# Query rotation inside the projection's bank, and routing logits from the product that turns a tile back

## The reference, cut to what matters

```python
h = _layernorm(x) * (1 + ca) + sa
q = rmsnorm(einsum('bim,mhd->bhid', h, wq)); k = rmsnorm(einsum('bim,mhd->bhid', h, wk))
even, odd = split(q, 2, axis=-1)                       # the same for k
q = concatenate([even * cos - odd * sin, even * sin + odd * cos], axis=-1)
p = softmax(q @ k.T / 128 + causal mask); x = x + ga * (p @ v @ wo)
h = _layernorm(x) * (1 + cb) + sb
scores = softmax(h @ Wr + br); top_idx = top_k(scores, 2)
weights = softmax(where(chosen, scores, -inf))
x = x + gb * sum_e(weights_e * (gelu(h @ W1_e + b1_e) @ W2_e + b2_e))
```

## Time and profile before

| | |
|---|---|
| median of three runs | 1145.86 us (1144.65 to 1147.39) |
| span of the profiled execution, first to last instruction | 1104.4 us |
| PE busy | 1019.0 us, 92% |
| ScalarE busy | 969.8 us, 88% |
| VectorE busy | 923.8 us, 84% |
| GpSimd busy | 825.8 us, 75% |
| mean granted clock of PE | 0.969 |

### The profile page before, as it was taken

How to read it: one execution, slowest core, us unless ns; L and a number is a source line. 1 busy time by engine, 2 the same in 40 slices (tenths; PEclk the granted TensorE clock), 3 DMA queues, 4 the chain that set the end, 5 groups by cost and what they waited for, 6 DMA issues and landing times. The chain is left out here.

```text
span 1104.4 us, 27346 instructions
## 1 busy us (share of the span) xinstructions
PE 1019.0 (92%) x7434; PEld 791.3 (72%) x7434; DVE 923.8 (84%) x2706; ACT 969.8 (88%) x3517; POOL 825.8 (75%) x1197
## 2 busy tenths in 40 slices
PE   5899999999999999999999999999989999999800
PEld 3478888888888888888888888888865455579600
DVE  4888999989999999888888888888766997778837
ACT  6899999999999999999999999999769999999534
POOL 6665578888888888888878788888745687777744
PEclk9999999999999999999999999999999999999955
DMA  5320000001000000000000000000034233321158
GB/s 150 104 71 14 13 18 23 23 26 34 27 23 26 26 23 14 16 16 16 14 15 16 14 14 16 16 16 16 16 111 129 84 118 104 96 85 40 46 207 261
DMA packets 53704, 57.90 MB, mean 52 GB/s; under 512 B 7964, under 2 KB 42639, under 8 KB 53556
## 3 DMA queue, kind: packets, MB, share of 16 engines
q1 hardware_dynamic: 36468, 35.10, 10.9%
q0 software_dynamic: 8640, 16.87, 4.4%
q10 hardware_dynamic: 8448, 4.20, 1.3%
HBM read 33.08 MB, written 23.97 MB: 52 GB/s over the span
## 5 line engine op out<-in xcount | busy, mean ns | idle before, releaser
L751 ACT ACTIVATE squares<-unit 128x128 f32<-128x128 f32 x1024 | 273.0, 302 | 3.6 <-PE unit L1211 3.4
L563 POOL TENSOR_TENSOR roped<-roped,rope_b 128x512 f32<-128x512 f32 x132 | 174.9, 1326 | 93.8 <-DVE rope_b L1099 91.4
L751 ACT ACTIVATION_READ_ACCUMULATOR squares<-unit 128x1 f32 x1024 | 234.1, 235 | 0.0
L1080 DVE TENSOR_TENSOR roped<-unit,cos_sb 128x512 f32<-128x512 f32 x256 | 174.4, 681 | 31.7 <-ACT squares L751 30.9
L1563 POOL DMA_INDIRECT y_rows<-y_out,place_y x142 | 155.3, 1093 | 54.3 <-issue 40.5
L1099 DVE TENSOR_TENSOR rope_b<-unit,sin_sb 128x512 f32<-128x512 f32 x256 | 174.3, 681 | 0.0
L729 ACT ACTIVATE probs<-scores,rr 128x256 f32<-128x256 f32 x256 | 123.7, 483 | 51.6 <-issue 25.5
L1291 PEld LDWEIGHTS unit<-ident,roped 128*128 128x128 f32 x1024 | 117.9, 142 | 31.9 <-ACT k_t L768 13.1
L1049 DVE SCALAR_TENSOR_TENSOR acc<-pv,den,acc 128x128 f32<-128x128 f32 x448 | 139.0, 341 | 0.3
L1291 PE MATMUL unit<-ident,roped 128*128 128x128 f32 x1024 | 135.2, 275 | 1.7 <-POOL roped L563 1.6
L572 POOL TENSOR_TENSOR roped<-roped,rr 128x1024 f32<-128x1024 f32 x64 | 121.6, 1900 | 9.6 <-DVE roped L1108 8.8
(11 more groups left out here) (310 smaller groups left out, 2972.3 us busy)
## 6 DMA issues: line engine op xcount, KB each, us to landing
shared<-y_rows SPq DMA_DIRECT2D x16, 512.0 KB, 5.6
x_all<-in_L_attn_x SPq DMA_DIRECT2D x32, 128.0 KB, 2.1
h_late<-in_L_ffn_W SPq DMA_DIRECT2D x16, 256.0 KB, 3.5
out_x<-hidden ACTq DMA_DIRECT2D x16, 256.0 KB, 4.4
rope_b<-x_rows SPq DMA_DIRECT2D x13, 258.0 KB, 2.9
tile_x<-x_rows SPq DMA_DIRECT2D x12, 258.0 KB, 3.0
y_rows<-y_out,place_y POOLq DMA_INDIRECT x142, 2.3
ga_b<-mod_dram SPq DMA_DIRECT2D x32, 64.0 KB, 2.9
```

What stands on the lines that cost most here:

```text
L563: pool.tensor_tensor(out=roped[parity][:, u, heads], in0=roped[parity][:, u, heads], in1=rope_b[:, u % 2, heads], op=ALU.add)\
L751: nc.scalar.activation(squares[:, c * D:(c + 1) * D], UN[0][:, c * D:(c + 1) * D], ACT.Square, accum_out=ssq[parity][:, u * H + c:u * H + ...
L1080: nc.vector.tensor_tensor(out=roped[parity][:, u, heads].rearrange("p (g c) -> p g c", c=D // 2), in0=UN[0][:, heads].rearrange("p (g c) - ...
```

## The change

For queries from pass 1 on, VectorE makes the sines first, then writes the cosine products back over the projection in its PSUM bank, and adds that bank and `rope_b` into `roped`. PE's projection waits for that add (`q_added`) two steps on, for steps 2 to 5. Keys, and pass 0, stay as they were.

The tile `ident_wr` holds the identity and, beside it, the routing weights. One f32 product of each tile of `h2_t` with these 136 columns gives the rows and the logits together, in steps 1 and 2 (`ROUTED`), beside the values products of heads 0 and 1. The turns of steps 4 and 5 and the group of one-row and 8-column products go. VectorE adds the bias, held in all partitions in `br_all` (one more load), to each tile's logits into the old place in `OP[0]` (`BIASED0`, `BIASED1`). Its later routing steps move: the maxima and `LESS_TOP` from step 1 to 2, `E_SUM` and `E_REC` from 3 to 4, some of the next by a slot; ScalarE's exponential moves from step 2 to 3, and GpSimd's score behind its low part of `h`. The diff leaves out the names of semaphores and most unchanged lines.

```diff
--- before.py
+++ after.py
@@ -84,7 +84,8 @@
         b_t = sb("b_t", [P, E * FC + E])
-        ident = sb("ident", [P, P])
+        ident_wr = sb("ident_wr", [P, P + E])
+        ident, wr_sb = ident_wr[:, 0:P], ident_wr[:, P:P + E]

@@ -96,10 +97,8 @@
         mod_t = sb("mod_t", [P, 4, NB])
-        wr_sb = sb("wr_sb", [P, E])
         br_sb = sb("br_sb", [1, TT * E])
-        br_rest = [sb(f"br_rest{k}", [1, TT * E]) for k in range(2)]
-        br_part = [sb(f"br_part{k}", [1, TT * E], BF16) for k in range(3)]
+        br_all = sb("br_all", [P, E])
         ones_row = sb("ones_row", [1, P])
@@ -293,7 +292,7 @@

-        (TOP_L0, TOP_L1, LESS_TOP, E_SUM, E_REC, TOP_S0, TOP_S1, TOP_I0, TOP_I1, ONE_HOT) = range(1, 11)
+        (BIASED0, BIASED1, TOP_L0, TOP_L1, LESS_TOP, E_SUM, E_REC, TOP_S0, TOP_S1, TOP_I0, TOP_I1, ONE_HOT) = range(1, 13)
         STEPS = ONE_HOT
@@ -302,8 +301,9 @@
         XN_AT, XN2_AT = 2, 3
-        BESIDE, TURN_AT = 2 * P + 8, 3 * P
+        BESIDE, TURN_AT = 2 * P + 8, 3 * P - E
         BACK_AT = {H_AT: 1, H_AT + 1: 0}
+        ROUTED = {1: 0, 2: 1}
         HH = H // 2
@@ -391,6 +391,8 @@
                     .then_inc(S["router_in"], 16)
+            sp.dma_start(br_all[:, :], br.rearrange("(o e) -> o e", o=1).broadcast_to([P, E]))\
+                .then_inc(S["router_in"], 16)
             sp.dma_start(b_rows[0:E * FC, :], b1.rearrange("e (k p) -> (e k) p", p=P)).then_inc(S["b_in"], 16)
@@ -626,18 +628,18 @@
                     scatter(n - 6, parity, 0, 0)
+                if X:
+                    b = n + 1
+                    wait(pool, "hhi_done", b + 1)
+                    wait(pool, "vw_done", TT * (b - 1))
+                    pool.tensor_tensor(out=h_lo[other][:, :], in0=h_t[:, :], in1=h_hi[other][:, :], op=ALU.subtract)\
+                        .then_inc(S["h_ready"], 1)
                 if RT:
...
                                        op=ALU.mult).then_inc(S["scored"], 1)
-                if X:
-                    b = n + 1
-                    wait(pool, "hhi_done", b + 1)
-                    wait(pool, "vw_done", TT * (b - 1))
-                    pool.tensor_tensor(out=h_lo[other][:, :], in0=h_t[:, :], in1=h_hi[other][:, :], op=ALU.subtract)\
-                        .then_inc(S["h_ready"], 1)
                 if A:
@@ -775,7 +777,7 @@
                             .then_inc(S["guess_done"], 1)
-                    if RT and h == 2:
+                    if RT and h == 3:

@@ -817,8 +819,7 @@
                         if not late:
-                            wait(act, "rt_done", b)
-                            wait(act, "h2_back", TT * b)
+                            wait(act, "rt_done", TT * b)
                         nc.scalar.activation(h2_late[:, b - LAST, :] if late else h2_t[:, :], UN[1][:, 0:T],
@@ -879,21 +880,13 @@

-                dve.wait_ge(S["router_in"], 16 * (TT + 1))
-                nc.vector.tensor_copy(br_part[0][:, :], br_sb[:, :]).then_inc(S["br_parted"], 1)
-                for k in range(2):
-                    whole = br_rest[0] if k else br_sb
-                    dve.wait_ge(S["br_parted"], 2 * k + 1)
-                    nc.vector.tensor_tensor(out=br_rest[k][:, :], in0=whole[:, :], in1=br_part[k][:, :],
-                                            op=ALU.subtract).then_inc(S["br_parted"], 1)
-                    dve.wait_ge(S["br_parted"], 2 * k + 2)
-                    nc.vector.tensor_copy(br_part[k + 1][:, :], br_rest[k][:, :]).then_inc(S["br_parted"], 1)
+                dve.wait_ge(S["router_in"], 16 * (TT + 2))
                 dve.wait_ge(S["b_turned"], 1)
...
             ROUTE = {
-                (1, 0): (TOP_L0, TOP_L1), (1, 1): (LESS_TOP,), (3, 3): (E_SUM,), (3, 4): (E_REC,),
-                (5, 0): (TOP_S0, TOP_S1), (5, 1): (TOP_I0,), (5, 2): (TOP_I1,),
+                (1, 1): (BIASED0,), (2, 0): (BIASED1,), (2, 1): (TOP_L0, TOP_L1), (2, 3): (LESS_TOP,),
+                (4, 0): (E_SUM,), (4, 1): (E_REC,), (5, 1): (TOP_S0, TOP_S1), (5, 2): (TOP_I0,), (5, 3): (TOP_I1,),
                 (6, 1): (ONE_HOT,)}
@@ -956,10 +949,14 @@
                     lg = OP[0][:, BESIDE:BESIDE + TT * E].rearrange("p (t e) -> p t e", t=TT)
-                    if step in (TOP_L0, TOP_L1):
+                    if step in (BIASED0, BIASED1):
+                        t = step - BIASED0
+                        wait(dve, "rt_done", TT * b + t + 1)
+                        ins = nc.vector.tensor_tensor(out=lg[:, t, :], in0=OP[t][:, TURN_AT + P:TURN_AT + P + E],
+                                                      in1=br_all[:, :], op=ALU.add)
+                    elif step in (TOP_L0, TOP_L1):
                         t = step - TOP_L0
-                        if t == 0:
-                            alone(dve, "rt_done", b + 1)
+                        after(BIASED0 + t)
                         ins = nc.vector.max(top_l[:, t, :], lg[:, t, :])
@@ -1020,7 +1017,7 @@
                     b, t = n - 5, BACK_AT[h]
-                    wait(dve, "h2_back", TT * b + h - H_AT + 1)
+                    wait(dve, "rt_done", TT * b + t + 1)
                     if (not isinstance(b, int) or b >= 2) and h == H_AT:
@@ -1064,34 +1061,23 @@
                     heads = slice(bank * HH * D, (bank + 1) * HH * D)
-
-                    adds, ended = (C, (n - 2, h - 1)) if h else (R, (n - 3, H - 1))
-                    if adds:
-                        denominators(*ended)
-                    small(h, 0)
-                    if ST and h == 2:
-                        place_e_step()
-                    if ST and h == 3:
-                        place_step()
-                    if A:
-
-                        wait(dve, "sq_done", HH * (w + 1))
-                        wait(dve, "tr_done", NU * (n - 1))
+                    in_place = h < HH and n > 0
+
+                    def cosines():
+
+                        if in_place:
+                            wait(dve, "rope_done", w + 1)
+                        else:
+                            wait(dve, "tr_done", NU * (n - 1))
+                        turned = UN[0][:, heads] if in_place else roped[parity][:, u, heads]
                         nc.vector.tensor_tensor(
-                            out=roped[parity][:, u, heads].rearrange("p (g c) -> p g c", c=D // 2),
+                            out=turned.rearrange("p (g c) -> p g c", c=D // 2),
                             in0=UN[0][:, heads].rearrange("p (g c) -> p g c", c=D // 2),
...
                             op=ALU.mult).then_inc(S["ropea_done"], 1)
-                    small(h, 1)
-                    if adds:
-                        add_head(*ended, 0)
-                    small(h, 2)
-                    if RT and h in BACK_AT:
-                        copy_rows(h)
-                    if adds:
-                        add_head(*ended, 1)
-                    small(h, 3)
-                    if A:
+
+                    def sines():
+
                         if h < HH:
@@ -1102,11 +1088,39 @@
                             op=ALU.mult).then_inc(S["rope_done"], 1)
-                    if A and h < HH and n > 0:
-
-                        wait(dve, "rope_done", w + 1)
-                        nc.vector.tensor_tensor(out=roped[parity][:, u, heads], in0=roped[parity][:, u, heads],
+
+                    adds, ended = (C, (n - 2, h - 1)) if h else (R, (n - 3, H - 1))
+                    if adds:
+                        denominators(*ended)
+                    small(h, 0)
+                    if ST and h == 2:
+                        place_e_step()
+                    if ST and h == 3:
+                        place_step()
+                    if A:
+                        wait(dve, "sq_done", HH * (w + 1))
+                        if in_place:
+                            sines()
+                        else:
+                            cosines()
+                    small(h, 1)
+                    if adds:
+                        add_head(*ended, 0)
+                    small(h, 2)
+                    if RT and h in BACK_AT:
+                        copy_rows(h)
+                    if A and in_place:
+                        cosines()
+                    if adds:
+                        add_head(*ended, 1)
+                    small(h, 3)
+                    if A and in_place:
+                        wait(dve, "ropea_done", w + 1)
+                        wait(dve, "tr_done", NU * (n - 1))
+                        nc.vector.tensor_tensor(out=roped[parity][:, u, heads], in0=UN[0][:, heads],
                                                 in1=rope_b[:, u % 2, heads], op=ALU.add).then_inc(S["q_added"], 1)
+                    elif A:
+                        sines()
                     small(h, 4)
@@ -1223,11 +1237,15 @@
                     o, pr, v = OP[h % 2], probs[:, h % NPR, :], vals[parity]
-                    if RT and h + 1 in BACK_AT:
-                        t = BACK_AT[h + 1]
+                    if RT and h + 1 in ROUTED:
```

(69 more changed lines are left out.)

6 lines of the change are left out of this document (1 added, 5 removed).

## The result

| | before | after |
|---|---|---|
| median, both kernels side by side | 1146.62 us (1144.17 to 1155.59, 8 runs) | 1134.12 us (1131.1 to 1142.35, 8 runs) |
| ratio | | 0.990 (0.987 to 0.993) |
| the same on a later occasion | 1106.15 us (15 runs) | 1094.35 us (4 runs) |
| ratio there | | 0.990 (0.988 to 0.991) |
| late logits start (end of attention) | 813.41 us | 801.42 us |

The change saves 1.0%: 12.5 us by the medians here, 11.8 on the later occasion. It lies in attention: the late logits start 12.0 us earlier.

A forecast was written before the change was run, and what follows sets the result against it. PE's instruction stream was taken to bound the attention pass: 0.56 us saved, less 0.17 at head 7 and 0.03 at LESS_TOP, left 0.36 to 0.38. 28 x 0.38 = 10.6 us off 1145.86 gave 1135.2 us, range 1130 to 1146.

The forecast's parts named there:

- PE's stream bounds the pass, and the net of its products is 0.56: Attention loop: a pass is as long as PE's instructions; 0.81 + 0.22 - 0.47 = 0.56 us less a pass.
- Wide products: PE, steps 1 and 2: two f32 products of 136 columns, 0.235 us each, 0.47 together.
- Late next is the accumulation of head 5, and it costs 0.17: Before head 7's values product PE waits 0.11 us for VectorE's accumulation and shows 0.06 of weight load.
- Cosines over the bank: VectorE, query rotation: writing into the bank costs between -0.01 and +0.1 us extra for 512 columns; 0 taken.
- rival C: Query rotation: reading and writing one bank takes 0.53 us extra; +5 us in all, 1151; chance 0.11.
- D: Rival, wide products: four 0.11 us steps a tile, 0.88 in all; 4 us saved, 1142; chance 0.03.
- LESS_TOP: VectorE, head 2: done 2.32 us after the reciprocal, PE needs it by 2.41; stall 0 to 0.15, 0.03 taken.
- The release of the projection's bank: Projection of head 5: bank released later, with the query add, at 526.62; in time by 0.3 us, 0 in the sum.
- None of this is on the path: in heads 0 to 3 VectorE waits for PE or ScalarE anyway.: Query rotation on VectorE, heads 0 to 3: its changed operation times do not affect the pass; 0 taken.
- rival A: VectorE not late, gaining more from adds no longer sharing SBUF with POOL: 16 to 17 us, 1129; chance 0.17.
- VectorE works without a gap through heads 4 to 6: VectorE, from 527.31 until head 5's accumulation ends: unbroken work, 0.25 us earlier, that accumulation moving from 534.27 to 534.02.
- the 41.5 us: Whole kernel: difference between span 1104.4 us and median 1145.86, taken as fixed time around the span.

The follow-up runs named there:

- the repeat: The whole change run once more on the later occasion, against the kernel before: 1094.35 us, ratio 0.990, passes of 24.16 us.
- the delayed kernel: The changed kernel with three added 128x8 copies on VectorE in front of LESS_TOP in head 2: 1134.76 us, 1.026 of the kernel before.
- rotation alone: The kernel before with only the query rotation through the bank, routing as before: 1106.59 us, ratio 1.001, passes of 24.57 against 24.56.
- ONE_HOT late: The changed kernel with ONE_HOT moved behind the accumulation of head 5: 1091.02 us, 0.987 of the kernel before, passes of 24.00.

## Why the prediction held, point by point

**Right.** *PE's stream bounds the pass, and the net of its products is 0.56*: with the edge at head 7 cleared, passes fall by 24.56 - 24.00 = 0.56. *Wide products* at 0.235 each: 0.23 for the first; the second shows 0.31 to what follows, but the extra 0.08 stood in the same place before, behind the first values product of head 1 (519.70 to 520.00 in the kernel before). *Waits on PE at 0*: the first wide product starts on the beat. *Late next is the accumulation of head 5, and it costs 0.17*: it is that edge, and it costs 0.14 (0.07 of wait where 0.11 was forecast, 0.07 of weight load for 0.06); moving one operation off it brings passes to 24.00, delaying it costs one to one. *Cosines over the bank*: two groups of one kernel, into SBUF and into the bank,

```profile
L1073 DVE TENSOR_TENSOR roped<-unit,cos_sb 128x512 f32<-128x512 f32 x132 | 89.7, 679 | 25.6 <-ACT squares L753 25.2
L1073 DVE TENSOR_TENSOR unit<-unit,cos_sb 128x512 f32<-128x512 f32 x124 | 85.7, 691 | 0.2
```

differ by 12 ns, so rival C (0.53 more) is out, and D falls with the two instructions of a wide product. Passes are 0.41 shorter, where 0.36 to 0.38 were forecast; the sum took the upper end, though its own terms (0.56 - 0.17 - 0.03) make 0.36. Between head 0's scores of pass 5 and pass 32 the 27 passes save 11.2 us of the 12.0; what comes behind takes 0.2 more. The other 0.95 lies ahead of pass 5: its scores stood at 117.01 in this trace, at 117.96 in the one before and at 118.67 in the repeat, so it is chance, no gain.

**Mis-sized.** LESS_TOP: 2.32 forecast from the reciprocal, 2.26 measured; I gave it 0.04 of slack and 0.03 of stall, and it has 0.20 and none. LESS_TOP itself was 0.06 earlier, and PE needs it 0.10 later: I placed that at the start of the weight load, 0.11 ahead of the product, with 0.05 for the signal, and the delayed kernel shows 0.06 in all. At head 7 the same reckoning fitted (0.11 + 0.04 against 0.147). The release of the projection's bank, with 0.3 of slack, showed no wait.

**Wrong.** *"None of this is on the path: in heads 0 to 3 VectorE waits for PE or ScalarE anyway."* True of the kernel before (rotation alone: 0), false of the one the change makes: without the new rotation 3.6 us of the 11.8 are missing. I read the idle time in front of VectorE's reciprocals and cosines as cover, and made the pass 0.4 us shorter around nearly the same VectorE work in the same sum; a slow add of 1.2 to 2.4 us then lasts longer than the cover that is left. The prediction named those adds in rival A, and dismissed them since heads 4 to 6 hold none; but they act from head 2, by using up the idle time in front of head 4.

**Missed altogether.** In "VectorE works without a gap through heads 4 to 6", ONE_HOT stands between 527.31 and the accumulation at 533.67, and I took its time as its work. The timeline of VectorE in the kernel before:

```profile
533.20 0.55 DVE L988 TENSOR_TENSOR one_hot<-iota_e,top_i 128x32 f32<-128x32 f32 x1
```

It held VectorE for 533.67 - 533.20 = 0.47 us, against 0.10 in the kernel with ONE_HOT late (523.46 to 523.56), where GpSimd's add is just ending: 0.37 was waiting. In the kernel after it is 0.62 and 0.52, since it starts 0.62 instead of 0.77 us into GpSimd's add. A stretch without idle time is not a stretch of work only. The group's duration against its size (532 ns for 128x32, where `lg_m` with 128x16 takes 166) would have shown some 4 us more to be had.

**At the root of the sum**: the 41.5 us, as said above.

## What to carry to other kernels

When an edit shortens the bounding engine, recount the slack of every engine that had idle time: a cost that was hidden before is priced by what is left of it, and the parts of a change are then worth more together than apart. Compare each small operation's duration with its size: one that lasts as long as another engine's overlapping operation is waiting, not working, and moving it by one place may be worth more than the change. And probe an edge with operations whose own duration cannot stretch, with an input in PSUM, or read their stretched duration before drawing a conclusion.

## What the runs showed of the hardware

- An operation of VectorE with two SBUF inputs is held until GpSimd's overlapping one is about over, and then takes its own length: 128x32 took 0.67, 0.42 or 0.19 us by its place, the query add 0.69 or, held, 1.58 and 1.79. GpSimd's next operation suffers in turn (0.72 for 0.25). With one input in PSUM the query add took 683 ns on average beside the same GpSimd work, 895 before.
- SBUF to SBUF copies of 128x8 are held as well: three took 0.51, 0.62, 1.28 or 1.67 us, and 0.21 to 0.22 of the last two were their own. The Trainium skill ("SBUF — State Buffer", Who interferes with whom) puts copies in a two-port mode under the same lock; that these ran in such a mode no run here shows. In head 4 they end at 505.90, behind GpSimd's 0.66 us operation at 505.15; how much of their 0.51 is the lock was not measured by itself.
- A late VectorE release costs PE more than the wait: 0.07 to 0.10 us of weight load that is otherwise hidden, at both edges in front of a values product. In front of the projection of step 6 (0.18 of wait, 507.55) none shows: the next product follows on the beat, at 507.77.
- The same expert stage took 291 us in one execution and 329 in another, at the same instruction counts and granted clock (0.89).
